# A three-part layer on one Trainium2 core: the turn of the quantised FFN hidden rows goes behind gate and up, and the values are weighed in four row groups of the array

## What is computed

```python
x = x + xattn(layernorm(x), ctx, ctx)  # 16 heads of 64, causal mask added as -10000
x = x + attn(layernorm(x))             # 16 heads of 16, causal
x = x + ffn(layernorm(x))              # 704 hidden, FP4 in blocks of 16

def ffn(x):                            # fp4_linear quantises both operands first
    h = silu(fp4_linear(x, w_gate)) * fp4_linear(x, w_up)
    return fp4_linear(h, w_down)
```

## Time and profile before

| what | value |
|---|---|
| median of 3 runs | 612.41 us (612.39 to 614.93) |
| the profiled execution, its own time | 609.85 us |
| its span | 608.4 us |
| PE, busy share of the span | 90% |
| DVE, busy share | 82% |
| ACT, busy share | 37% |
| POOL, busy share | 7% |
| TensorE clock granted, mean | 0.972 of full |

### The profile page before, as it was taken

One profiled execution on the slowest core, in us unless ns is written; L12 is line 12 of the kernel. 1 busy time (PEld: TensorE's weight loads), 2 busy tenths in 40 slices (PEclk: granted clock), 3 DMA queues, 4 the chain that ended last, 5 costly groups with the idle time before them and its releaser, 6 DMA issues. The chain is left out here.

```text
span 608.4 us, 15957 instructions
## 1 busy us (share of the span) xinstructions
PE 548.6 (90%) x6390; PEld 431.9 (71%) x6390; DVE 498.2 (82%) x955; ACT 223.4 (37%) x461; POOL 45.0 (7%) x84
## 2 busy tenths in 40 slices
PE   4999999999999999999627799999999999999975
PEld 4888898888889888888516557776666666676644
DVE  4868999999999999999718588889888888888863
ACT  1333232223323222332114645554444455554221
POOL 4001000000000000000012111111111011110100
PEclk9999999999999999999967999999999999999987
DMA  8991111210111111012100000000000000000000
GB/s 249 334 287 43 69 69 69 69 50 19 69 69 69 69 69 55 18 65 70 70 4 0 4 2 10 0 9 9 9 9 9 9 9 9 9 9 9 11 9 18
DMA packets 13798, 30.97 MB, mean 51 GB/s; under 512 B 976, under 2 KB 10704, under 8 KB 11728
## 3 DMA queue, kind: packets, MB, share of 16 engines
q1 hardware_dynamic: 13776, 30.67, 15.4%
HBM read 28.57 MB, written 2.10 MB: 50 GB/s over the span
## 5 line engine op out<-in xcount | busy, mean ns | idle before, releaser
L321 PEld LDWEIGHTS bank<-x_xcT,xwk 128*128 128x128 f32 x512 | 61.6, 198 | 2.8 <-issue 1.1
L321 PE MATMUL bank<-x_xcT,xwk 128*128 128x128 f32 x512 | 62.0, 281 | 1.4 <-ACT x_xcT L413 1.4
L343 PE MATMUL bank<-xwv,x_xcT 128*128 128x512 f32 x128 | 59.2, 605 | 1.2
L312 PE MATMUL bank<-x_xcT,xwq 128*128 128x128 f32 x512 | 59.8, 275 | 0.0
L362 PE MATMUL bank<-xwo,x_oT 128*128 128x256 f32 x256 | 58.0, 379 | 0.9 <-ACT x_oT L430 0.9
L312 PEld LDWEIGHTS bank<-x_xcT,xwq 128*128 128x128 f32 x512 | 58.5, 192 | 0.0
L362 PEld LDWEIGHTS bank<-xwo,x_oT 128*128 128x128 f32 x256 | 47.5, 190 | 7.2 <-issue 1.4
L1109 PE MATMUL bank<-wdT,f_hqT 128*128 128x256 f32 x192 | 47.6, 399 | 3.0 <-ACT f_hqT L1229 3.0
L1258 ACT ACTIVATE a_kblocks<-bank,head_rows 128x256 f32<-128x256 f32 x128 | 48.6, 499 | 0.0
L442 ACT COPY x_k_blocks<-bank 64x512 f32<-64x512 f32 x32 | 18.6, 580 | 80.9 <-PE bank L321 80.7
L539 DVE STREAM_TRANSPOSE x_probsT<-x_probs 32x512 f32<-32x512 f32 x64 | 44.9, 701 | 1.7
(11 more groups left out here) (147 smaller groups left out, 947.8 us busy)
## 6 DMA issues: line engine op xcount, KB each, us to landing
x_ctx_slab<-in_ctx_dram SPq DMA_DIRECT2D x16, 1028.0 KB, 4.8
out_dram<-f_out SPq DMA_DIRECT2D x16, 128.0 KB, 1.7
xall<-in_x_dram SPq DMA_DIRECT2D x1, 1280.0 KB, 17.4
x_first_keys<-in_ctx_dram SPq DMA_DIRECT2D x4, 320.0 KB, 13.0
xwk<-in_L_xattn_w_k_dram SPq DMA_DIRECT2D x1, 1024.0 KB, 5.0
xwq<-in_L_xattn_w_q_dram SPq DMA_DIRECT2D x1, 1024.0 KB, 7.1
xwv<-in_L_xattn_w_v_dram SPq DMA_DIRECT2D x1, 1024.0 KB, 10.5
xwo<-in_L_xattn_w_o_dram SPq DMA_DIRECT2D x1, 1024.0 KB, 13.0
```

What stands on the lines that cost most here:

```text
L312: last = nc.tensor.matmul(bank67[:, j // 4, (j % 4) * P:(j % 4 + 1) * P], xwq[:, k, j * P:(j + 1) * P], xcT[:, k, :], start=(k == 0), stop ...
L321: last = nc.tensor.matmul(bank[2 + j // 4][:, (j % 4) * P:(j % 4 + 1) * P], xwk[:, k, j * P:(j + 1) * P], xcT[:, KD + k, :], start=(k == 0 ...
L343: last = nc.tensor.matmul(bank45[:, half, :], xcT[:, KD + k, :], xwv[:, k, half * 512:(half + 1) * 512], start=(k == 0), stop=(k == KD - 1))
```

## The change

In the first stage, `pT` shrinks from 128 by 128 a head to 128 by 32: each of its four row blocks holds one sequence's turned probabilities, with no zeros around them. `turn_probs` becomes a single transpose over all 128 partitions, and the clearing of pT at the start goes. `weigh` issues four matmuls for a head, each with 32 rows of the array, at tile positions (32b, half), with 32 columns moving, and the four write four different PSUM banks, 2 to 5; that makes 64 matmuls in place of 16. As banks 2 and 3 hold the next tile's keys, weigh now waits for both `spread_k(t+1)`. `copy_o` reads the four banks and reorders.

In the second stage, `turn_h` and ACT's `copy_h` move behind gate and up (ACT: behind the grid of x), in every step. The turned rows go to bank 2, which scores has used, and to half of bank 0; the down product goes to an unused quarter of bank 5. New waits: turn_h for the shift (`s_a_sh`) and for ACT's copy of xn (`s_n_xc`), down_product for the hidden product (`s_f_h`) of tile t - 2, gate_up for `add_out(t - 4)` (`s_f_out`) and for `s_f_h`. Gone: gate_up's wait for copy_h, and scores' wait for `s_f_out`.

```diff
-        bank = [ctx.enter_context(nc.psum_tensor(f"bank{i}", [P, 512], F32)) for i in range(4)]
-        bank45 = ctx.enter_context(nc.psum_tensor("bank45", [P, 2, 512], F32))
+        bank = [ctx.enter_context(nc.psum_tensor(f"bank{i}", [P, 512], F32)) for i in range(2)]
+        bank2345 = ctx.enter_context(nc.psum_tensor("bank2345", [P, 4, 512], F32))
+        bank += [bank2345[:, 0, :], bank2345[:, 1, :]]
+        bank45 = bank2345[:, 2:4, :]
...
-            pT = psb("probsT", [P, H, P])
-            oT = psb("oT", [P, XP, P])
+            pT = psb("probsT", [P, H, SQ])
+            oT = psb("oT", [P, XP, BT, SQ])
...
-                    def weigh(t):
+                    def weigh(t, spread):
                         pe.wait_ge(s_p, t + 1)
                         pe.wait_ge(s_vc, t + 1)
+                        if spread is not None:
+                            pe.wait_ge(s_kc, spread + 1)
+                            pe.wait_ge(s_kca, spread + 1)
+
                         for h in range(H):
                             j, half = h // 2, (h % 2) * XD
-                            last = nc.tensor.matmul(bank45[half:half + XD, j // 4, (j % 4) * P:(j % 4 + 1) * P],
-                                                    v[:, h * XD:(h + 1) * XD], pT[:, h, :],
-                                                    start=True, stop=True, tile_position=(0, half))
+                            for b in range(BT):
+                                rows = slice(b * SQ, (b + 1) * SQ)
+                                last = nc.tensor.matmul(bank2345[half:half + XD, b, j * SQ:(j + 1) * SQ],
+                                                        v[rows, h * XD:(h + 1) * XD], pT[rows, h, :],
+                                                        start=True, stop=True, tile_position=(b * SQ, half))
...
-                            last = nc.tensor.matmul(bank67[:, 0, 0:D], oT[:, j, :], xwo[:, j, :],
-                                                    start=(j == 0), stop=(j == XP - 1))
+                            last = nc.tensor.matmul(bank67[:, 0, 0:D], oT[:, j].rearrange("p b q -> p (b q)"),
+                                                    xwo[:, j, :], start=(j == 0), stop=(j == XP - 1))
...
-                        weigh(t)
+                        weigh(t, t + 1)
...
                     def copy_o(t):
                         act.wait_ge(s_o, t + 1)
-                        nc.scalar.copy(oT[:].rearrange("p (a j) n -> p a (j n)", a=2), bank45[:]).then_inc(s_oc, 1)
+                        nc.scalar.copy(oT[:].rearrange("p j b q -> p b j q"),
+                                       bank2345[:, :, 0:XP * SQ].rearrange("p b (j q) -> p b j q", q=SQ))\
+                            .then_inc(s_oc, 1)
...
                     def turn_probs():
-                        for b in range(BT):
-                            rows = slice(b * SQ, (b + 1) * SQ)
-                            step(nc.vector.transpose(pT[rows, :, rows], pr[rows, :, :]))
-                        dve.sem_inc(s_p, 1)
+                        nc.vector.transpose(pT[:], pr[:]).then_inc(s_p, 1)
...
-                    nc.vector.memset(pT[:], 0.0)
...
-            def h_bank(t, half):
...
-                if isinstance(t, int) and t == T - 3:
-                    return bank[2][:, D:2 * D] if half else bank[3][:, :]
-                if isinstance(t, int) and t == T - 2:
-                    return bank[half][:, :]
-                return bank45[:, half, :]
+            h_bank = (bank[2], bank[0][:, 2 * P:])
+            down_bank = bank45[:, 1, 2 * P:2 * P + D]
...
-                    def scores(t, added):
-                        if added is not None:
-                            pe.wait_ge(s_f_out, added)
+                    def scores(t):
...
-                    def turn_h(t):
-                        if isinstance(t, int) and t == T - 3:
-                            pe.wait_ge(s_f_out, t + 1)
+                    def turn_h(t, shifted, turned):
+
+                        if shifted is not None:
+                            pe.wait_ge(s_a_sh, shifted)
+                        if turned is not None:
+                            pe.wait_ge(s_n_xc, turned)
                         pe.wait_ge(s_f_hq, t + 1)
...
-                    def down_product(t, shifted):
+                    def down_product(t, gated):
                         pe.wait_ge(s_f_hc, t + 1)
-                        if shifted is not None:
-                            pe.wait_ge(s_a_sh, shifted)
-                        else:
-                            pe.wait_ge(s_f_out, t + 1)
+                        pe.wait_ge(s_f_out, t + 1)
+                        if gated is not None:
+                            pe.wait_ge(s_f_h, gated)
                         for c in range(FC):
-                            last = nc.tensor.matmul(bank[2][:, 0:D], f_hqT[:, c, :], wdT[:, c, :],
+                            last = nc.tensor.matmul(down_bank, f_hqT[:, c, :], wdT[:, c, :],
...
-                    def gate_up(t, copied):
+                    def gate_up(t, added):
                         pe.wait_ge(s_f_xc, t + 1)
-                        if copied is not None:
-                            pe.wait_ge(s_f_hc, copied)
+                        if not (isinstance(t, int) and t == 0):
+                            pe.wait_ge(s_f_h, t)
+                        if added is not None:
+                            pe.wait_ge(s_f_out, added)
...
                         if gate:
                             turn_xq(t - 2, attend)
-
-                        late_gate = gate and not attend
-                        if norm and not attend:
-                            output(t - 1)
-                        if down and not late_gate:
-                            turn_h(t - 3)
-                        if norm and attend:
+                        if norm:
                             output(t - 1)
...
                         if project:
                             turn_xn(t + 1)
                         if gate:
-                            gate_up(t - 2, t - 2 if down and not late_gate else None)
-                        if late_gate:
-                            turn_h(t - 3)
+                            gate_up(t - 2, t - 2 if down else None)
+                        if down:
+                            turn_h(t - 3, t + 1 if attend else None, t + 2 if project else None)
                         if project:
                             project_qk(t + 1)
                         if attend:
                             values(t)
                         if down:
-                            down_product(t - 3, t + 1 if attend else None)
+                            down_product(t - 3, t - 1 if gate else None)
...
-                        if down:
-                            copy_h(t - 3)
...
                             grid(f_xn[:], f_grid_x[:], s_f_xs, s_f_xg, t - 1)
+                        if down:
+                            copy_h(t - 3)
                         if project:
                             copy_qk(t + 1)
```

More of the change, by code:

```diff
@@ L393, in _ @@
                     project_q(T - 1)
-                    weigh(T - 2)
+                    weigh(T - 2, T - 1)
                     scores(T - 1)
@@ L397, in _ @@
                     output(T - 2)
-                    weigh(T - 1)
+                    weigh(T - 1, None)
                     pe.wait_ge(s_reach, 1)
@@ L579, in _ @@
                     start = Chain(dve, s_ln, 3 * len(PARTS))
-                    step = Chain(dve, s_d, 2 + 1 + 3 + BT)
+                    step = Chain(dve, s_d, 2 + 1 + 3)
                     slab_step = Chain(dve, s_dc, 1)
@@ L1090, in turn_h @@
                             m = P if c < FC - 1 else FR
-                            last = nc.tensor.transpose(h_bank(t, c // 4)[0:m, (c % 4) * P:(c % 4 + 1) * P],
+                            last = nc.tensor.transpose(h_bank[c // 4][0:m, (c % 4) * P:(c % 4 + 1) * P],
                                                        f_hq[:, c * P:c * P + m], ident[:])
@@ L1181, in step @@
                         if attend:
-                            scores(t, t - 2 if down else None)
+                            scores(t)
                         if gate:
                             turn_xq(t - 2, attend)
-                        late_gate = gate and not attend
-                        if norm and not attend:
-                            output(t - 1)
-                        if down and not late_gate:
-                            turn_h(t - 3)
-                        if norm and attend:
+                        if norm:
                             output(t - 1)
@@ L1323, in add_out @@
                         dve.wait_ge(s_stored, 16 * t + 16)
-                        nc.vector.tensor_tensor(f_out[:], bank[2][:, 0:D], tile_of(t), ALU.add).then_inc(s_f_out, 1)
+                        nc.vector.tensor_tensor(f_out[:], down_bank, tile_of(t), ALU.add).then_inc(s_f_out, 1)
```

6 lines of the change are left out of this document (3 added, 3 removed).

## The result

The changed kernel takes **606.8 us** as the median of 4 runs (603.78 to 607.31), the kernel before 613.23 (612.39 to 614.93) beside it: a ratio of 0.989, 95% interval 0.9848 to 0.9933. So it is faster by 1.1%, 6.4 us. The forecast was 12.6 us less, about twice what was measured; 606.8 lies in the range, near its slow end. The two profiled executions took 603.78 and 609.85 us, so they show 6.1 us of difference, and each is about 3 us under its own median.

A forecast was written before the change was run, and what follows sets the result against it. PE was taken to bound the first stage, a closed loop of PE and DVE the second. Terms -11.4 - 3.3 + 0.6 - 0.5 + 2.0 = -12.6 us gave 599.8 us against the median, range 594.5 to 608.

The forecast's parts named there:

- weigh's size: First stage, 16 times: weigh falls from 1.90 to 1.19 us, priced from values, 11.4 us gained in all.
- In the loop that buys nothing by itself, PE being the bound: First stage: turn_probs as one transpose saves DVE 2.2 us a tile, but no time in the loop by itself.
- The row group rivals: First stage's weigh: row groups over the same columns load in turn, 3.8 us each, about 641 us in all; chance 0.07.
- two halves take turns: First stage's weigh: halves' loads alternate, 1.9 us as now, 611 to 613 in all; half of a chance of 0.20.
- The between case: First stage: weigh ends up between, 1.5 to 2.0 us; at 1.5, 605 in all; half of a chance of 0.20.
- The Trainium skill's rule: First stage's weigh: about 60 cycles overhead a matmul, an estimated 3.2 us for weigh and 632 us in all.
- The last tile: End of the first stage: PE's 3.31 us wait for the turned probabilities goes, 3.3 us gained.
- copy_o: First stage, ACT: same number of elements in another order, taken as unchanged at 1.01 us.
- The second stage's pass: Second stage, 12 times: wait moves from turn_h to turn_xn, pass 16.14 us for 16.09, 0.6 us lost.
- The residual's wait: Second stage, DVE: output comes forward, so the 0.46 us wait before the residual goes, once, 0.5 us gained.
- the second stage does gain: Second stage: PE alone sets its pass at 15.1 us, giving 588 us in all; chance 0.07.
- The tail: Steps 16 and 17: gate of tile 15 waits for add_out of tile 13, 2.0 us lost.

The follow-up runs named there:

- e10: e7 with weigh sending all 16 pairs of a position one behind the other; 717.99 us, ratio 1.1701.
- e8: e5 with each matmul of weigh moving 16 of its 32 columns, half the queries' weighed values left out; 596.35 us, one run.
- e9: e7 with weigh's loops nested so that the two halves of a row group follow each other directly; 583.17 us, ratio 0.9523.
- e4: The changed kernel with SP holding back the loads of the FFN weights, and what follows them, until copy_o of tile 0; 600.96 us, ratio 0.9835.
- e3: The changed kernel with add_out of tile 13 in step 16 placed ahead of the grid of the hidden rows on DVE; 600.82 us, ratio 0.9823.
- e1: The first stage's part of the change alone, against the kernel before; 606.1 us, ratio 0.9904.
- e6: e5 with DVE's normalise_n of tile t + 1 ahead of taking the scores out of PSUM; 586.63 us, ratio 0.9582.
- e7: e5 with normalise_n computed for tile t + 2, ahead of add_out, and step 14 written out behind the loop; 581.42 us, ratio 0.9519.
- e5: The changed kernel with the edits of e3 and e4 together; 595.94 us, ratio 0.9748.

## Why the prediction was right, and where it was not

The parts that were named did move, most of them as forecast, but that the time fell in the range is partly luck: weigh's size and an unforeseen stop cost 8.4 us against the sum, and a gain of 3.0 us in the second stage, which was not forecast either, brought the time back in. Without it the median would have been about 610 (an estimate, 606.8 + 3.0), above the range.

**weigh: the mechanism was right, the term was mis-sized.** The prediction took 1.19 us from values, with 0.86 as the lower bound. It is 1.41, 11.0 ns a pair instead of 9.3. That is a gain of 0.49 us in each of 15 passes and 0.33 in the last, 7.7 us, where 11.4 stood in the sum: 3.7 us of the 6.5 that are missing. The lower bound stood on eight positions that load side by side, each taking its 16 pairs in turn. e10 bears out the price of a position, 58 ns a pair, and the first 32 pairs keep the pace of eight positions side by side (a stretch of the changed kernel, weigh's instructions alone, with the columns length, PE, PEld, DVE, clock, DMA share and GB/s: 33 weight loads in 0.24 us, 7.3 ns each, an eighth of 58):

```profile
194.37:194.61 0.24, 0.23 (x30) 0.23 (x33) 0.00 (x0) 1.00 0.00 0
```

The other 96 need 1.17 us: behind the 32nd pair stands a pause of 58 ns, then the starts are 8.3 ns apart on average for most and 17 ns for some. The row that the price was taken from has the same step: in values, before, the starts from the 33rd pair on are 8.5 ns apart on average, but it has no such pause and no rows of starts 17 ns apart. So the price of 9.3 ns a pair left out the pause and the 17s. e8 shows that moving columns don't do that, e9 that putting the two halves of a row group next to each other doesn't. What hands the later pairs over so slowly stays open; it isn't in any wait that the trace names.

**turn_probs was worth more than the prediction said.** "In the loop that buys nothing by itself, PE being the bound" took DVE's pass for PE's: the 17.70 us from shift to shift are DVE's list, without a wait for another engine in them, and PE's pass was 17.75. With DVE's list as it was, weigh's 0.49 us could have shortened the pass by an estimated 0.05 only. The 2.2 us that turn_probs saves let the pass follow weigh down to 17.26. This is worked out from the timelines; no run has the new weigh with the old turn_probs.

**The row group rivals fell.** Two row groups over the same columns do overlap: at 58 ns a pair one behind the other weigh would be near 4 us, and it is 1.41. The "two halves take turns" rival has its trial in e9, where it would have been 1.9 us and is 1.42. The between case, at 1.5 to 2.0 us, begins just above what was measured. The Trainium skill's rule in TensorEngine Tiling (Array Packing), Performance Considerations, of about 60 cycles for every matmul, made 3.2 us of weigh and an estimated 632 us of the whole; the trace, with 11.0 ns a pair on eight positions, disagrees with it.

**The stop in the first pass was not seen at all.** 4.65 us with the lower clock behind it. The prediction counted weigh's instructions as time in the array and not as a list that PE has to be given, four times as long, just when the FFN's weights are being loaded (the inferred cause, see e4). No row of before shows such a stop, but the DMA's load in that stretch was there to be read. e4 gets most of it back: its first pass is 18.11 us, 0.85 over the others. In e3 and e1 the loss is larger than here, with first passes of 23.23 and 23.52 us, as the lower clock lasts 6.8 us there and not 3.4.

**The last tile: right.** 3.3 us forecast, 3.07 measured (3.31 to 0.24). turn_probs takes 701 ns, and no spread_k holds weigh up in the loop. **copy_o: right**, 1.01 us.

**The second stage's pass: right in its mechanism, a little too dear.** The wait went from turn_h to turn_xn, as forecast, 1.00 us long, and e6 and e7 show the loop through normalise_n, turn_xn and add_out by shortening it and opening it: 0.59 and 1.22 us a pass less. The pass became 15.91 and not 16.14. The difference is in three terms: from turn_xn to gate it is 0.27 us (0.38 taken), from gate to up 2.37 (2.44 before), turn_h 0.66 (0.71 taken); 0.23 in all. Over 12 passes 2.2 us gained instead of 0.6 lost. The residual's wait is gone, once, at the loop's entry (0.5 forecast, 0.74 measured together with the shorter pass).

**The rival "the second stage does gain" was within reach.** Its 15.1 us of PE's own work were even too much: e7's pass, with no wait in it, is 14.69. What stood against it, the order of DVE's list, was the one obstacle.

**The tail: right.** 2.0 us lost forecast, 2.2 measured, by the wait that was named, and up kept its clock. What the prediction took for granted was that gate's low clock is a price of this stage: e3 shows that it goes with the wait.

**First start, +0.53 us**, was not in the sum; it varies by more than that between the kernels here (the first weigh starts between 33.4 and 34.7), so nothing is concluded from it.

In the sum: -12.6 forecast, -6.1 in the profiles. weigh's size makes +3.7 of the difference, the stop +4.65, the start and the way into the second stage +0.8, the last tile and the tail +0.4, and the second stage gives back 3.0.

## What to carry to other kernels

Where the passes of two engines differ by 0.05 us, as PE's and DVE's did in the first stage, a gain on the one needs a gain on the other; look at whether the second engine has any wait at all before calling the first the bound. Small matmuls on different positions of the array overlap and on one position they don't, so go round the positions; but price them by the nearest row with the same load, and count the longer instruction list too, above all where a loop's first pass runs beside bulk loads. When a wait moves to another instruction and the pass stays, write down the closed loop between the two engines: one operation of 0.4 us taken out of it was worth 14 us here, more than the whole change. And after a change of a shared bank look at the written-out tail, where the order of the loop doesn't hold and a PE that waits can fall to the lower clock (here with 2.23 and 3.65 us of waiting).

## What the hardware showed that was not expected

- Pairs of load and matmul on eight positions start 7.3 ns apart on average for the first 32, then, after a pause of 58 ns, mostly 8.3 and some 17 ns, whatever the columns moving (16 or 32) and whichever half comes next. On one position they start 58 ns apart, and 26 to 32 around a change of position, but for one start of 6 ns there. The Trainium skill, TensorE: Matmul & The Clock Gate, in the section on 56 and 53.3 ns, has starts never nearer than about 25 ns; e10's rows agree but for that start of 6 ns, those on eight positions, at 7.3 ns, don't.
- PE stood still for 3 us with no semaphore behind it while the DMA engines were full, and for under 1 us when they weren't (0.59 us in e4), always behind the 123rd pair. The stop ended 1.3 to 1.5 us after the end of a 16 KB transfer of the instruction queue. In e5, and in e10 with its slower pairs, weigh gets to that instruction only after that time, and there is no stop. In e4 to e9, with the loads held back, the first pass is 17.3 to 18.3 us.
- The granted clock fell to 1.2 GHz in e10 while PE was never idle: it was issuing pairs on one position at a time, 3.70 us busy of 3.70. In the tail it fell while PE idled for 3.65 us, and in the kernel before while it idled for 2.23 us; with 0.63 us (e3) it didn't.
